# Eight tiles of exponentials, second products in a stream of their own, and ternary weights held once

## The reference

```
x = x + attention(layernorm(x))    # 16 heads of 8 channels; softmax over 1024 keys of a group
x = x + ternary_ffn(layernorm(x))
x = x + gla(layernorm(x))          # gated linear attention: a scan over the 1024 tokens
x = x + zones(layernorm(x))        # router: 3 of 8 experts per batch row

# attention: Q, K, V = x @ w + b, reshaped to (B * 16, 1024, 8)
scores = einsum("bqd,bkd->bqk", Q, K) / sqrt(8)
ctx    = einsum("bqk,bkd->bqd", softmax(scores), V)
out    = layernorm(ctx @ wo + bo + x) * gamma + beta
# ternary_ffn: the weights of w1, w2, h1, h2, w3 are -1, 0 or 1, with a scale per output
h = silu(x @ w1.T * s1) * (x @ w2.T * s2)
h = gelu(h @ h1.T * sh1);  h = gelu(h @ h2.T * sh2);  out = h @ w3.T * s3
```

## Time and profile before

| | |
|---|---|
| time, median of 3 runs | 1035.55 us (1034.36 to 1039.66) |
| the profiled execution | 1037.2 us, its span 1034.9 us, 2.3 us around it |
| mean granted clock of PE | 0.987 of 2.4 GHz |
| first scores, last scores, end of the span | 27.26 us, 761.6 us, 1034.9 us |
| busy of the span | PE 93%, ACT 79%, DVE 70%, POOL 34% |

### The profile page before, as it was taken

How to read it: one execution, slowest core, us unless ns; L and a number is a source line. 1 busy time by engine, 2 the same in 40 slices (tenths; PEclk the granted TensorE clock), 3 DMA queues, 4 the chain that set the end, 5 groups by cost and what they waited for, 6 DMA issues and landing times.

```text
span 1034.9 us, 16677 instructions
## 1 busy us (share of the span) xinstructions
PE 966.3 (93%) x5859; PEld 454.0 (44%) x5859; DVE 720.5 (70%) x1276; ACT 813.3 (79%) x1058; POOL 356.4 (34%) x309
## 2 busy tenths in 40 slices
PE   3999999999999999999999998999899999999998
PEld 1232235333533452346233533453347666566666
DVE  5223855567488778777888887688699998997300
ACT  0899888988889989999899898989976485644542
POOL 1000102114322435343625342534554465546100
PEclk8899999999999999999999999999999999999999
DMA  6855244065216533651266136412342322252020
GB/s 158 194 145 139 72 122 116 32 141 148 62 61 166 134 81 92 147 146 58 62 157 171 53 93 179 128 43 75 92 105 82 97 84 82 74 145 68 12 71 21
DMA packets 140998, 106.26 MB, mean 103 GB/s; under 512 B 92848, under 2 KB 107984, under 8 KB 140880
## 3 DMA queue, kind: packets, MB, share of 16 engines
q1 hardware_dynamic: 135984, 102.78, 37.3%
q10 hardware_dynamic: 4896, 1.87, 0.7%
HBM read 75.25 MB, written 29.36 MB: 101 GB/s over the span
## 4 chain that ended last, share of the span: by engine, by line
PE 47%; ACT 16%; DVE 16%; issue 11%; DMA 4%; POOL 4%; SPq 1%; ACTq 0%; DVEq 0%; POOLq 0%
PE PS L1488 14%; ACT R L909 9%; PE PS L1451 9%; PE PS L1535 7%; DVE R L1264 4%; DVE R L1255 4%; PE PS L1662 4%; DMA R<-VD 3%; ACT L883 3%; PE PS L1650 3%; PE PS L1575 2%; PE PS L1597 2%; PE PS L1606 1%; POOL R L854 1%; DVE RB L1220 1%
## 5 line engine op out<-in xcount | busy, mean ns | idle before, releaser
L909 ACT ACTIVATE R<-PS 128x1024 f32<-128x1024 f32 x512 | 487.2, 1042 | 55.9 <-PE PS L1451 54.2
L1488 PE MATMUL PS<-R 128*32 128x512 f32 x2048 | 293.5, 611 | 1.0 <-DVE R L1208 0.9
L854 POOL TENSOR_TENSOR R<-R 128x512 f32<-128x512 f32 x128 | 189.8, 1489 | 185.5 <-ACT R L985 126.0
L1451 PE MATMUL PS<-RA 32*128 32x512 f32 x1024 | 181.3, 500 | 29.0 <-ACT R L909 23.4
L1264 DVE TENSOR_TENSOR_SCAN R<-R 128x512 f32<-128x512 f32 x128 | 186.0, 1453 | 2.3
L1451 PEld LDWEIGHTS PS<-RA 32*128 32x128 f32 x1024 | 70.6, 183 | 255.3 <-ACT R L909 164.4
L1535 PE MATMUL PS<-RB,WR 128*128 128x512 f32 x640 | 175.7, 416 | 5.3 <-POOL RB L840 2.7
L1535 PEld LDWEIGHTS PS<-RB,WR 128*128 128x128 f32 x640 | 115.3, 189 | 69.0 <-issue 29.5
L883 ACT ACT_TABLE_LOAD x84 | 107.8, 1283 | 35.6 <-PE PS L1535 12.8
L1255 DVE TENSOR_TENSOR R<-R 128x512 f32<-128x512 f32 x128 | 118.5, 926 | 22.7 <-DMA R<-VD 18.5
L840 POOL TENSOR_TENSOR RB<-R,RB 128x512 fp32r<-128x512 f32 x48 | 74.9, 1560 | 164.6 <-DVE RB L1220 164.6
(11 more groups left out here) (127 smaller groups left out, 856.6 us busy)
## 6 DMA issues: line engine op xcount, KB each, us to landing
R<-VD SPq DMA_DIRECT2D x128, 256.0 KB, 4.1
RA<-QD SPq DMA_DIRECT2D x64, 256.0 KB, 4.4
QD<-RA SPq DMA_DIRECT2D x56, 256.0 KB, 3.9
RA<-QD SPq DMA_DIRECT2D x64, 128.0 KB, 4.3
OD<-R SPq DMA_DIRECT2D x32, 256.0 KB, 2.1
R<-OD SPq DMA_DIRECT2D x128, 32.0 KB, 2.5
R<-in_Wa SPq DMA_DIRECT2D x12, 256.0 KB, 3.7
R<-in_Wb SPq DMA_DIRECT2D x12, 256.0 KB, 4.2
```

What stands on the lines that cost most here:

```text
L854: pool.tensor_tensor(st, st, Qc, ALU.mult).then_inc(S["qh"], 1)
L909: act.activation(PR[u % 4], bank(2 * s, 1024), ACT.Exp, scale=SC).then_inc(S["exp"], 1)
L1451: op = pe.matmul(bank(2 * s + h), exact(KS[k][p:p + 32, 128 * j:128 * j + 128]), exact(QS[k][p:p + 32, :]), start=True, stop=stop)
L1488: op = pe.matmul(bank(ob)[c:c + 32, :], VAF[b % 2][:, at:at + 32], PR[u % 4][:, 512 * h:512 * h + 512], start=(j == 0), stop=(j == 7), til ...
```

## The change

1. There are eight tiles of exponentials (`NP`), so exp of u waits for the second product of u - 8.
2. The second products are a stream `y` of their own, a round per step. `ORDER` is new throughout: it says how far they lag, and often puts two rounds of them one behind the other.
3. `WR` holds each ternary weight once, as it is. The weights are copied from DRAM to DRAM first (`WD`), all eleven at once, and then loaded straight into `WR`; DVE still does the three steps per weight, but into scratch tiles and for the flag alone. The first step waits for all 22 transfers.
4. `products` branches ahead of the first matmul; the arm for weights that aren't exact makes the whole sum in fp32, the other the whole sum in fp32r as before. The latter is what runs.

```diff
+NP = 8
     def stream_x(self):
         ...
             for w in range(8):
-                u = 16 * pr + 2 * w
-                self.add("scores", u)
+                self.add("scores", 16 * pr + 2 * w)
                 yield
-                if u >= 2:
-                    self.add("weigh", u - 2)
-                    self.add("weigh", u - 1)
-                if w == 0 and pr:
-                    self.add("finish", pr - 1)
-                    self.acc = pr
+
+    def stream_y(self):
+
+        for pr in range(32):
+            for w in range(8):
+                self.add("weigh", 16 * pr + 2 * w)
+                self.add("weigh", 16 * pr + 2 * w + 1)
+                if w == 7:
+                    self.add("finish", pr)
+                    self.acc = pr + 1
                 yield
...
-    "qqqqwxxxxxxxxxxxqxxxxxxlxxxxxxxxxxxxxxxwxwxxwxlxxxxxxwxxxfxxxqxxwfxwxxlxxwqqxwxxwxxxxxlxxwxxxxxfwxxx"
+    "wwwwxwwwwxxqqyxyxyxyqxwyxqlxyywxwyxyyxqxyxqxyqxyxyywfxywlxyxyxyxyxyxwylfxwywxwyxyxyxwyxywxyxylxyqwxy"
...
             def load_weights(n):
-                if n:
-                    need.wait_ge("w_split", n)
-                sp.dma_start(Wt if n < 10 else W3, io["wB"][n]).then_inc(S["w_in"], 16)
+                if n == 0:
+                    for m in range(11):
+                        sp.dma_start(WD[m, :, :], io["wB"][m]).then_inc(S["w_in"], 16)
+                    return
+                need.wait_ge("w_in", 16 * 11)
+                for m in range(0 if n == 1 else n, n + 1):
+                    sp.dma_start(weight(m) if m < 10 else W3, WD[m, :, :]).then_inc(S["w_in"], 16)
...
                     need.wait_ge("scores", u + 1)
-                    if u >= 4:
-                        need.wait_ge("pv", u - 3)
-                    act.activation(PR[u % 4], bank(2 * s, 1024), ACT.Exp, scale=SC).then_inc(S["exp"], 1)
+                    if u >= NP:
+                        need.wait_ge("pv", u - NP + 1)
+                    act.activation(PR[u % NP], bank(2 * s, 1024), ACT.Exp, scale=SC).then_inc(S["exp"], 1)
...
             def weights(n):
-                need.wait_ge("w_in", 16 * (n + 1))
+                need.wait_ge("w_in", 16 * 22)
...
-                for n, (i, k) in enumerate(seq):
-                    w, x, ev = terms[k]
-                    need.wait_ge(*ev[i])
-                    op = mm(w(0), x(i), start=(n == 0), stop=(n == len(seq) - 1))
-                    if n == 0:
-                        with pe.If_eq(ternary, 1):
...
+                with pe.If_eq(ternary, 1):
+                    sums(need.inner(), True)
+                with pe.Else():
+                    sums(need, False)
```

More of the change, by code:

```diff
@@ L31 @@
[L31 to L35, removed]
@@ L245, in stream_w @@
             yield
+        for n in range(11):
             self.add("weights", n)
@@ L506, in build, with weight @@
         bo4 = sb("bo4", [128, 3, 128])
-        with nc.sbuf_tensor("WR", [128, 2, 11, 512], F32R) as WR:
+        with nc.sbuf_tensor("WR", [128, 11, 512], F32R) as WR:
             pass
-        WP = sb("WP", [128, 11264])
+        WP = sb("WP", [128, 5632])
         W3 = WP[:, 5120:5632]
+        def weight(n, c0=0, c1=512):
+            return WR[:, n, c0:c1].bitcast(F32)
         wmx = sb("wmx", [128, 16])
@@ L562, in build @@
         QS = [kq[:, 1024:1536] for kq in KQ]
-        PR4 = carve(4096)
-        PR = [PR4[:, 1024 * i:1024 * i + 1024] for i in range(4)]
+        PRF = carve(1024 * NP)
+        PR = [PRF[:, 1024 * i:1024 * i + 1024] for i in range(NP)]
         VAF = [carve(1040) for _ in range(2)]
@@ L1171, in weights @@
                     return
-                own.step(dve.tensor_copy(WR[:, 0, n, :], Wt))
+                if n:
+                    need.wait_ge("w_split", n)
+                own.step(dve.tensor_copy(part(Wt), weight(n)))
                 own.settle()
-                own.step(dve.tensor_tensor(WR[:, 1, n, :], Wt, WR[:, 0, n, :], ALU.subtract))
+                own.step(dve.tensor_tensor(TT, weight(n), part(Wt), ALU.subtract))
                 own.settle()
-                dve.tensor_reduce(wmx[:, n:n + 1], WR[:, 1, n, :], AX.X, ALU.max,
+                dve.tensor_reduce(wmx[:, n:n + 1], TT, AX.X, ALU.max,
                                   apply_absolute_value=True).then_inc(S["w_split"], 1)
@@ L1529, in ternary_begin, with products, sums, half_of @@
                 need.wait_ge("w_split", 10)
-            def products(out_ap, terms):
-                def mm(w, x, **kw):
-                    return pe.matmul(out_ap, w, x, **kw)
+            def products(out_ap, terms, done):
                 seq = [(i, k) for i in range(2) for k in range(len(terms))]
-                for n, (i, k) in enumerate(seq):
-                    w, x, ev = terms[k]
-                    need.wait_ge(*ev[i])
-                    op = mm(w(0), x(i), start=(n == 0), stop=(n == len(seq) - 1))
-                    if n == 0:
-                        with pe.If_eq(ternary, 1):
[L1543 to L1547, removed]
+                def sums(waits, whole):
+                    for n, (i, k) in enumerate(seq):
+                        w, x, ev = terms[k]
+                        waits.wait_ge(*ev[i])
+                        op = pe.matmul(out_ap, w(whole), x(i, whole), start=(n == 0), stop=(n == len(seq) - 1))
+                    op.then_inc(S[done], 1)
+                with pe.If_eq(ternary, 1):
+                    sums(need.inner(), True)
+                with pe.Else():
+                    sums(need, False)
             def wpart(n, c0, c1):
-                return lambda j: WR[:, j, n, c0:c1]
+                return lambda whole: weight(n, c0, c1) if whole else WR[:, n, c0:c1]
+            def half_of(x):
+                return lambda i, whole: part(x[:, i, :]).bitcast(F32) if whole else part(x[:, i, :])
             def gate_mm(b, m, evs, ba, bb, g1, g2):
@@ L1554, in gate_mm @@
                 room(ba)
[L1555 removed]
+                products(bank(ba), [(wpart(0, 128 * m, 128 * m + 128), half_of(x), evs)], "gate_ps")
                 emptied[ba] = g1
                 room(bb)
[L1558 removed]
+                products(bank(bb), [(wpart(1, 128 * m, 128 * m + 128), half_of(x), evs)], "up_ps")
                 emptied[bb] = g2
@@ L1563, in hid_mm @@
                 room(bk)
-                terms = [(wpart(n0 + k, 128 * m, 128 * m + 128), (lambda i, k=k: part(xs[k][:, i, :])), evs[k]) for k in range(4)]
-                products(bank(bk), terms).then_inc(S["hid_ps"], 1)
+                terms = [(wpart(n0 + k, 128 * m, 128 * m + 128), half_of(xs[k]), evs[k]) for k in range(4)]
+                products(bank(bk), terms, "hid_ps")
                 emptied[bk] = hi
```

47 lines of the change are left out of this document (24 added, 23 removed).

## The result

The kernel after takes **1028.5 us** (median of 14 runs, 1023.4 to 1033.8), the kernel before 1036.7 beside it (14 runs): ratio 0.991, 95% interval 0.989 to 0.993. The sign of the forecast holds, its size doesn't: 8 us instead of 18.

The account below looks back on a forecast made before the run. ACT was taken to bound the attention (645.4 of 712 us busy). 1037.2 - 18.6 - 3.9 + 2.6 + 1.7 = 1019.0 us profiled, 1017.4 as a median; forecast range 1008 to 1030 (chance 0.44), 8-in-10 range 994 to 1042.

Parts of the forecast that it names:

- Eight tiles and a stream of their own: Attention: second products moved behind scores save half of ACT's 37.2 us of waits for scores, -18.6 us.
- "A quarter" of the waits for ternary products: Attention: a quarter of the 15.7 us that ACT waits for ternary products goes, -3.9 us.
- Branch ahead of the sums: PE, 128 branches before ternary sums: between -0.6 and +1.3 us, taken as 0 because PE is busy with earlier work.
- Weights, and the branch itself: DVE's single wait for all weight loads, and PE's branch before the ternary sums: each counted as 0.
- Table loads: ACT: two more table loads up to the last exponential, +2.6 us.
- Start: SP's queue: weight copies delay pass 3's keys and queries, +1.7 us, between 0 and +21.
- Pairs: PE: two second-product rounds in a row save 0.12 us per neighbour, up to -6.2 us; counted 0 since ACT bounds.
- The stretch behind: From the last scores to the kernel's end: as long as before, 273 us.
- "No change": Rival: score waits come from ternary sums and `down` regardless, PE's wait only moves; put at 1036 us, chance 0.22.
- "Pairs starve ACT": Slower rival: scores plus two second-product rounds take PE 2.31 us against ACT's 1.84; put at 1045 us, chance 0.15.
- "Much faster": Rival: all 52.9 us of ACT's waits for scores and ternary products go; 987 at best, put at 998 us, chance 0.19.

Follow-up runs that it names:

- experiment 6: Kernel after, TensorE's not-taken guard pieces left out (1002.0 us): 27 pairs of second-product rounds taken apart, 1024.6 us; all rounds pulled to at most one behind their scores, 1046.4 us.
- experiment 2: Kernel after with the order list of the kernel before: 1041.6 us; the same with TensorE's not-taken guard pieces left out: 1033.1 us.
- the pair without pieces: Kernels after and before, each with TensorE's not-taken guard pieces (search for a block's largest score) left out: after 1002.0 us, before 1032.7 us.

## Why the prediction was right and wrong, step by step

- **Eight tiles and a stream of their own, "half" of 37.2 us: right in mechanism, size too large.** Without the stops the waits for scores fall from 35.9 to 23.9 us, -12.0 where -18.6 was forecast. That moved rounds are a cause is shown by experiment 6.
- **"A quarter" of the waits for ternary products: too small.** They go almost whole, 16.1 to 1.9 us (-14.2, forecast -3.9). My reason, that most of such a wait is the length of the sums, is refuted, for the sums are as long as before. Rounds of second products are part of it: 27 moved rounds bring the waits from 1.9 to 12.9 us. With all rounds back at one behind they are 5.9 us, though, so the new order of the other steps has a part too. Together with the first term 26.2 us were won, 22.5 forecast; that these sums come close is luck, as the two errors cancel.
- **The step that failed: "Branch ahead of the sums ... between -0.6 and +1.3; I take 0".** I priced the branch where it stands and read only the idle time in front of matmuls. A branch that isn't taken is also code, and code that is added or reordered moves every guard behind it within the packets. In the kernel after the guards cost 26.5 us, in before about 5: 21 us that no term of the sum had. No single edit has this price: the arm cost 11.5 us beside the guards and 1.4 without them. Without the stops the change is worth 30.7 us where the sum has 18.2, so the forecast was too small for what the list does and had nothing for the stops. That 1028.5 still lies in its 1008 to 1030 is luck: the two misses go opposite ways. The row that should have warned me was in the trace of before: L1428's branch with 3797 ns against a median of 210. The Trainium skill ("Runtime: NRT & Kernel Launch", section "Instruction fetch mechanics") says that a taken branch whose target is not in the instruction memory's present window must wait for a fetch of its 16 KB page. The traces agree as far as the wait goes, with up to 7.1 us for one branch.
- **Weights, and the branch itself, at 0: right.** On the old list these edits can't be told from noise without the pieces (experiment 2). DVE's single wait for all weights was 18.1 us long, and this shows no price of it.
- **Table loads, +2.6: right.** 61 instead of 59 up to the last scores.
- **Start, +1.7: about right, but it varies.** Pass 3's scores begin at 73.45 instead of 74.84, with PE waiting 1.4 us for keys. The first scores come 1.3 us earlier, so pass 3 is as late against them as before. In the pair without pieces pass 3 begins at 75.74 instead of 73.88, PE waits 3.8 us for keys, and ACT stands 3.5 us there instead of 0.8. SP's queue does hold pass 3 up, as the forecast says.
- **Pairs, 0.** Not measured alone; experiment 6 moved rounds to other company, which hides 0.12 us apiece.
- **The stretch behind, unchanged: right** (273.4 us).
- **The rivals.** "No change" fails: with as much PSUM as before the waits of 52.0 us fall to 25.8. The Trainium skill ("TensorEngine Tiling (Array Packing)", PSUM Bottleneck) says that the copy out of PSUM may become the bottleneck once tiling has made the products faster. No run here shows it as the bound. "Pairs starve ACT" fails by experiment 6. "Much faster" (998) is close to what the change does without the stops (1002.0), but not for its reason: 25.8 us of the waits are still there.

Still open is what makes the packet late: it begins between 1.8 us ahead of such a branch's start and 4.3 us behind it. The three latest fall where the DMA engines are full, which speaks for a queue behind data. But full engines ahead of the branch aren't enough for it, nor always there, as three windows of the kernel after show: the 2 us ahead of the branch at 88.1, ahead of the one at 647.3, and from there to the begin of its packet (the column before the last is the DMA share):

```profile
86.10:88.10 2.00, 2.00 (x20) 0.53 (x12) 1.97 (x4) 2.00 (x4) 0.00 (x0) 1.00 1.03 225
645.30:647.30 2.00, 2.00 (x17) 0.76 (x20) 1.97 (x5) 2.00 (x4) 1.33 (x1) 1.00 0.00 0
647.30:648.90 1.60, 0.65 (x8) 0.00 (x0) 1.45 (x3) 0.72 (x2) 1.52 (x2) 1.00 0.90 230
```

At 88.1 the engines were full, and the packet still began 1.2 us ahead of the branch. At 647.3 they had been idle, and the packet began 1.6 us into the branch, so it was asked for late, or went in behind data that came with the branch. No run separates the two.

## What to carry to other kernels

Code that doesn't run isn't free: read the longest compare-and-branch of each engine in the trace, not the median, and where a jump is about a code packet long, reckon with edits ahead of it that move the stop. Before a change of a few per cent is judged, compare both kernels without such jumps; here a difference of 8 us hid one of 31. In an order written out by hand, put work that isn't urgent where the queue is otherwise empty: beside other work each such round cost 0.84 us of its 1.00 here.

## What the runs showed of the hardware

- TensorE's branch takes 0.21 us as a median, and 1.0 to 7.1 us in 24 cases; each of these ended 1.3 to 1.6 us after a 16 KB code packet had ended.
- Code comes in 16 KB packets, and code that is jumped over takes its share of them: emptying eight guards saved eight packets in after (84 to 76) and nine in before (79 to 70). Whether a packet of nothing but such code is fetched, no run shows.
- A stop can drag on: in the 5.7 us behind one of 6.6 us PE's granted clock was 0.69.
